# Order of the last chunk's table work and of GpSimd's second table set in a four-stage sequence kernel

## The chip, the cores and the metric

The kernel runs on one core of a Trainium2 chip. The metric is the device time of one execution in microseconds (us); three runs of the kernel before are shown, and one more execution was taken with the hardware profiler.

## The reference

An input `x` of 128 rows x 64 channels x 1024 steps goes through four additions, each with per-row conditions:

```
x = x + einsum('bct,bcd->bdt', x, W0[ids0])            # stage 0: a 64x64 mix per row
x = x + mask1 * (causal_conv(x, K1) + x * D1)          # stage 1: state-space convolution
x = x + x @ W2.T + bias + scale * (x @ A.T) @ B.T      # stage 2: 1024x1024 weights and a low-rank part
x = x + mask3 * (causal_conv(x * mask3, K3) + ...)     # stage 3: a second state-space convolution
K[h, l] = 2 * Re( sum_n Ct[h, n] * exp(dtA[h, n] * l) )   # 64 heads, 64 terms, 1024 steps, for each convolution
```

## The kernel before, in words

Work is split over channels into 16 groups (`NG`) of four (`HG`). The four engines, and the sync engine (SP) that issues most transfers, each run their own hand-written list of steps; a step waits on counting semaphores, so what stands in front of a step on its own engine delays it too.

**Opening.** Stage 0 runs over eight blocks and stores its result in DRAM (`x1_scratch`). Beside it, the tables of both convolutions are made in eight chunks of 16 heads. A chunk is: VectorE's `right_angles`, `left_angles` and `adv_angles` (multiply by steps, round off whole turns), ScalarE's `chunk_sines` (sines, then exponentials), VectorE's `combine_a` and `combine_b`, which end in the semaphore `tables_ready`; then the chunk's table is stored (`store_tab`, to `tab_scratch`) and TensorE's `sum_k` makes the first kernel samples of it. Chunks 0 to 6 are done within stage 0. The eighth (`NBLK - 1`) is spread: its right angles and step 3 of its sines come after stage 0, its left angles stand on VectorE between the first and the second `t_split_lo(0, n)` (line 2116), its sine steps 5 and 6 on ScalarE behind the four `t_split_hi(0, n)` (line 1582), its combining on VectorE behind the low-rank rows of group 0 (line 2153), its store on ScalarE's queue behind the second pair of PSUM reads (line 1606).

**Group 0.** Stage 1's sums leave PSUM by `take_half` on VectorE (line 2043), are split into two float16 parts (`x2_split_hi` on ScalarE L1482, `x2_split_lo` on VectorE L2063), and `t_rows` (L2101 to L2106, counted by the semaphore `t_made` up to 4) makes the four combinations that a fast matrix product of stage 2 takes. `t_split_hi` (L1532) and `t_split_lo` (L2110) split these; `t_split_lo` n lets SP load a quarter of the next group's `x1` from DRAM (`load_part(1, n)`, line 567). TensorE's `stage2(0)` goes in order: own blocks, `low_products` (L1044), the two mixed blocks (L1068, they wait for `t_hi` and `t_lo` 1), the low-rank terms (L1077, they wait for `low_hi` and `low_lo`, which come from VectorE's scaling L2145, ScalarE's L1594 and VectorE's L2149), two sum blocks, `sum_k(NBLK - 1, 3)` (L818, waits for `tables_ready`), and then the blocks with `t_parts[2]`, which wait for `s2_read` 5.

ScalarE's list in `body(0)` is: low-rank high part, four PSUM reads (`read_part`, L1540), the store of the table, the difference row (L1608), two `x1_split_hi(1, h)` (L1473, these wait for the loaded quarters), and only then the `read_part` that gives `s2_read` 5. Later in the same list come `bases_hi(0, 1)` and on VectorE `bases_lo(0, 1)` (L1950), which lets SP load the next kernel rows and GpSimd go on.

**GpSimd** makes the tables of each group and convolution in `make_tables(v, g)`: six small products (L718 to L726, 128x68) and seven large ones (L728 to L744, 128x1024 or 128x512). In `body(0)` it makes (0, 1), then (1, 0), of which the second large product waits for `u_lo`, that is `bases_lo(0, 1)`. Table (0, 1) waits for its loaded rows alone.

Of the kernel before, what the change touches and what calls it, by code (L numbers as in the profile page):

```python
# [36 lines left out]
NBLK = T // P  # L37
# [12 lines left out]
HG = 4  # L50
# [28 lines left out]
def build(nc, x, ids0, len1, ids2, len3, w0, ssm1, ssm3, w2, bias2, lora_a, lora_b, lora_s, out):  # L79
    with ExitStack() as ctx:  # L80
# [12 lines left out]
        tab_dram = nc.dram_tensor("tab_scratch", [2 * NG, P, TAB], F32).ap()  # L93
# [62 lines left out]
        tab = [t.rearrange("p (q n) -> p q n", q=HG) for t in (part_of(gbuf, 16, HG * TAB / 256), area(48, HG * TAB / 256))]  # L156
# [90 lines left out]
        tables_ready = sem("tables_ready")  # L247
# [267 lines left out]
        def _(sp):  # L515
# [92 lines left out]
                load_tab(1, 0, n)  # L608
            for part in range(NPART):
                sp.wait_ge(x1_stored[1][part], 16 * NBLK // 2)  # L610
            def turn_x3(g, h):
                for part, xx in enumerate((x3h, x3l)):
                    sp.dma_start_transpose(x3t[:, h % 2, part], xx[:, h].rearrange("p k b -> p (k b)")).then_inc(x3_turned[h], 16)
# [56 lines left out]
        def _(pool):  # L670
# [28 lines left out]
            def make_tables(v, g):  # L699

                n = made(v, g)
                pool.wait_ge(tab_loaded[v], 32 * (g + 1))
                if v == 1:

                    at_least(pool, c3_past, HG * g)
                elif made_ahead(v, g):
                    pool.wait_ge(s2_summed, NSUM * (g - 1))
                    pool.wait_ge(x3_lo, NBLK * (g - 1))
                m32 = m32_first if is_first(v, g) else m32_ahead if made_ahead(v, g) else m32_late
                u32, v32, tab_now = base_home(v, g), table_home(v, g), tab_home(v, g)  # L710
                v4 = v32[:, :, 0:2, :].rearrange("p h n (a j) -> p h (n a) j", j=TB)
                m4 = m32.rearrange("p h (a j) -> p h a j", j=TB)
                u4 = u32.rearrange("p h (a j) -> p h a j", j=TB)
                at_least(pool, v_made, 2 * n)
                re, im = [tab_now[:, TAB - (2 - k) * HG:TAB - (1 - k) * HG].rearrange("p (h o) -> p h o", o=1).to_broadcast([P, HG, TL])
                          for k in range(2)]
                l0, l1, l2, l3, tmp = [left_row(tab_now, k) for k in range(5)]
                ptt(l2, l0, re, ALU.mult).then_inc(left_parts, 1)  # L718
                ptt(tmp, l1, im, ALU.mult).then_inc(left_parts, 1)
                ptt(l3, l1, re, ALU.mult).then_inc(left_parts, 1)  # L720
                pool.wait_ge(left_parts, 6 * n + 3)
                ptt(l2, l2, tmp, ALU.add).then_inc(left_parts, 1)
                pool.wait_ge(left_parts, 6 * n + 4)
                ptt(tmp, l0, im, ALU.mult).then_inc(left_parts, 1)
                pool.wait_ge(left_parts, 6 * n + 5)
                ptt(l3, l3, tmp, ALU.subtract).then_inc(left_parts, 1)  # L726
                pool.wait_ge(left_parts, 6 * n + 6)
                ptt(m4, left_of(tab_now, 2), right_of(tab_now, 0), ALU.mult).then_inc(u_parts, 1)  # L728
                at_least(pool, u_lo, n)
                ptt(u4, left_of(tab_now, 3), right_of(tab_now, 1), ALU.mult).then_inc(u_parts, 1)  # L730
                pool.wait_ge(u_parts, 2 * n + 2)
                ptt(u4, u4, m4, ALU.add).then_inc(u_made, 1)
                pool.wait_ge(u_made, n + 1)
                if is_first(v, g):
                    pool.wait_ge(tab_stored[0], 16 * NBLK // 2)
                ptt(m4, left_of(tab_now, 0), right_of(tab_now, 0), ALU.mult).then_inc(v_parts, 1)
                at_least(pool, v_lo, n)
                ptt(v4, left_of(tab_now, 1), right_of(tab_now, 1), ALU.mult).then_inc(v_parts, 1)
                pool.wait_ge(v_parts, 2 * n + 2)
                ptt(v4, v4, m4, ALU.add).then_inc(v_made, 1)  # L740
                decay = tab_now[:, 0:2 * LEFT].rearrange("p (s h a) -> p h s a", s=2, a=TL)[:, :, :, TB:TL].to_broadcast([P, HG, 2, C])
                eye = twin[:, :].rearrange("p (o s n) -> p o s n", o=1, s=1).to_broadcast([P, HG, 2, C])
                d4 = (v32[:, :, 2, :] if v == 0 else v32[:, :, 2, ::-1]).rearrange("p h (s n) -> p h s n", s=2)
                ptt(d4, eye, decay, ALU.mult).then_inc(v_made, 1)  # L744
# [28 lines left out]
            def body(g, more2):  # L773
                if isinstance(g, int) and g == 0:
                    for part in range(NPART):
                        pool.wait_ge(x1_stored[0][part], 16 * NBLK // 2)
                    make_tables(0, 1)
                make_tables(1, g)
                if more2:
                    make_tables(0, g + 2)  # L780
# [481 lines left out]
        def _(act):  # L1262
# [16 lines left out]
            def store_tab(c, r):  # L1279

                act.wait_ge(tables_ready, c + 1)
                act.dma_start(tab_dram[bass.ds(c * HG, HG)].rearrange("q p n -> p q n"), tab[r]).then_inc(tab_stored[r], 16)
# [40 lines left out]
            def chunk_sines(c, r, step):  # L1323

                if step == 3:
                    act.wait_ge(table_angles, 2 * c + 1)
                    nc.scalar.activation(right_slot(r, 0), right_slot(r, 0), ACT.Sin, bias=phase_cos, scale=-TURN)
                    nc.scalar.activation(right_slot(r, 1), right_slot(r, 1), ACT.Sin, scale=-TURN)
                if step == 5:
                    act.wait_ge(table_angles, 2 * c + 2)  # L1330
                    nc.scalar.activation(left_slot(r, 0), left_slot(r, 0), ACT.Sin, bias=phase_own, scale=-TURN)
                    nc.scalar.activation(left_slot(r, 1), left_slot(r, 1), ACT.Sin, bias=phase_adv, scale=-TURN)
                if step == 6:
                    nc.scalar.activation(angle_r, angle_r, ACT.Exp)
                    nc.scalar.activation(angle_l, angle_l, ACT.Exp).then_inc(table_sines, 1)
# [243 lines left out]
                x2_split_hi(0, h)  # L1579
            for n in range(4):  # L1580
                t_split_hi(0, n)
            chunk_sines(NBLK - 1, 1, 5)
            chunk_sines(NBLK - 1, 1, 6)
            for part in range(NPART):
                act.wait_ge(x1_stored[0][part], 16 * NBLK // 2)
                act.wait_ge(x1_stored[1][part], 16 * NBLK // 2)
# [1 line left out]
            def body(g, more1, more2):  # L1588
# [14 lines left out]
                read_part(g, 0, MIX_AT[0], 2, NQ, 2, 3)  # L1603
                read_part(g, 1, MIX_AT[1], 2, NQ, 2, 4)
                if early:
                    store_tab(NBLK - 1, 1)
                act.wait_ge(low_diff, g + 1)
                nc.scalar.activation(lowdh, lowf.rearrange("p h b -> p (h b)")[:, 0:HW], ACT.Copy).then_inc(lowd_hi, 1)  # L1608
                if more1:
# [83 lines left out]
        def _(dve):  # L1693
# [164 lines left out]
            def left_angles(c, r):  # L1858
                table_link(tt(four(angle_l), param(c, 1, TL), left_steps, ALU.mult), c, 7)
                round_off(left_slot(r, 0), four(angle_l), quarter_own, half_own[:, 0:1], half_own[:, 1:2], c, 8)  # L1860

            def adv_angles(c, r):
                table_link(round_off(left_slot(r, 1), four(angle_l), quarter_adv, half_adv[:, 0:1], half_adv[:, 1:2], c, 10), c, 12)
                tt(four(angle_l), param(c, 0, TL), left_steps, ALU.mult).then_inc(table_angles, 1)

            def combine_a(c, r):
                dve.wait_ge(table_sines, c + 1)
                at_least(dve, k_summed, c)
                tt(right_slot(r, 0), right_slot(r, 0), four(angle_r), ALU.mult)
                tt(left_slot(r, 0), left_slot(r, 0), four(angle_l), ALU.mult)  # L1870
                table_link(tt(right_slot(r, 1), right_slot(r, 1), four(angle_r), ALU.mult), c, 13)
                table_link(tt(left_slot(r, 1), left_slot(r, 1), four(angle_l), ALU.mult), c, 14)
                nc.vector.tensor_copy(four(turn_r)[0:C, :, :, ::-1], right_slot(r, 0)[0:C])
                nc.vector.tensor_copy(four(turn_r)[C:2 * C, :, :, ::-1], right_slot(r, 1)[C:2 * C])
# [233 lines left out]
            def t_split_lo(g, n):  # L2108
                dve.wait_ge(t_hi, 4 * g + n + 1)
                stt(t_part(n, 1), t_region(n), XS / FS, t_part(n, 0), ALU.mult, ALU.subtract).then_inc(t_lo, 1)  # L2110

            t_rows(0)
            for n in range(4):
                t_split_lo(0, n)
                if n == 0:
                    left_angles(NBLK - 1, 1)
                    adv_angles(NBLK - 1, 1)

            def past_sum(g, h):

# [18 lines left out]
            def body(g, more1, more2):  # L2139
# [10 lines left out]
                dve.wait_ge(low_lo, g + 1)  # L2150
                tt(low_row[:, 0:HW], low_row[:, 0:HW], low_row[:, HW:2 * HW], ALU.subtract).then_inc(low_diff, 1)
                if early:
                    combine_a(NBLK - 1, 1)
                    combine_b(NBLK - 1, 1)
                for h in range(HG):
# [124 lines left out]
```

## Time and profile before

| what | us |
|---|---|
| three runs: lowest, median, highest | 1560.33, 1564.65, 1567.99 |
| profiled execution, its own time | 1560.88 |
| span of its instructions | 1558.9 |
| busy: TensorE, VectorE, ScalarE, GpSimd | 1492.1, 1230.2, 752.9, 633.3 |
| mean granted clock of TensorE, share of full speed | 0.987 |

The span runs from the first to the last instruction; the own time has some 2 us around it. Line numbers are those of the kernel before. Times of day in the rows ("at 261.42") are us from the start of the span.

### The profile page before, as it was taken

What the parts mean: (1) busy time and instruction counts of PE and PEld (TensorE: products, weight loads), DVE (VectorE), ACT (ScalarE), POOL (GpSimd) and SP (SyncE); (2) the same over time, 40 slices, a digit from 0 to 9 for tenths busy, and PEclk for the clock granted to TensorE, in tenths of its full rate; (3) what the DMA queues carried; (4) which work ended last, traced back from release to release, by engine and by line L of the source; (5) the groups of instructions that cost most, each with busy time, mean ns of one, the idle gap of its engine ahead of it and who ended that gap; (6) DMA issues with size and microseconds to landing.
All of it is one profiled execution on the core that took longest, in us unless ns stands there. A gap on an engine that the chain in (4) does not pass through costs nothing.

```text
span 1558.9 us, 36859 instructions
## 1 busy us (share of the span) xinstructions
PE 1492.1 (96%) x14983; PEld 1292.4 (83%) x14983; DVE 1230.2 (79%) x1479; ACT 752.9 (48%) x1105; POOL 633.3 (41%) x455
## 2 busy tenths in 40 slices
PE   7888697999999999999999999999999999999998
PEld 7877685788888888888888888888888888888887
DVE  8888669788787969696969696978787887969653
ACT  4555543554444545454545454535454444445433
POOL 1211046445454545454443535353535454545040
PEclk9999899999999999999999999999999999999999
DMA  8899985848483848484848566674848583858432
GB/s 286 302 377 387 368 290 158 188 112 216 89 232 80 235 90 225 99 224 92 221 106 196 136 174 159 146 187 119 195 114 208 99 231 88 223 85 230 99 135 69
DMA packets 437847, 283.43 MB, mean 182 GB/s; under 512 B 330536, under 2 KB 377136, under 8 KB 437680
## 3 DMA queue, kind: packets, MB, share of 16 engines
q1 hardware_dynamic: 388784, 175.35, 47.7%
q10 hardware_dynamic: 48928, 106.00, 19.6%
q8 instruction: 119, 1.95, 0.5%
q14 instruction: 16, 0.13, 0.0%
HBM read 159.20 MB, written 73.86 MB: 150 GB/s over the span
## 4 chain that ended last, share of the span: by engine, by line
PE 76%; DVE 10%; DMA 6%; issue 4%; ACT 3%; ACTq 0%; DVEq 0%; SPq 0%
PE ps L1068 35%; PE ps L978 8%; PE ps L1168 7%; DMA arena<-in_x_dram 5%; PE ps L1077 5%; PE ps L1044 5%; PE ps L1014 4%; PE ps L1181 3%; PE ps L869 3%; PE ps L988 3%; DVE arena L2066 3%; PE ps L797 1%; DVE gbuf L2057 1%; ACT arena L1564 1%; ACT arena L1484 1%
## 5 line engine op out<-in xcount | busy, mean ns | idle before, releaser
L1068 PE MATMUL ps<-arena,w2t 128*128 128x256 f16 x4608 | 524.2, 273 | 7.4 <-ACT arena L1532 5.1
L1068 PEld LDWEIGHTS ps<-arena,w2t 128*128 128x128 f16 x4608 | 451.7, 98 | 65.0 <-ACT arena L1532 5.6
L718 POOL TENSOR_TENSOR arena<-arena 128x68 f32<-128x68 f32 x31 | 27.7, 893 | 665.7 <-DVE arena L2130 396.7
L2173 DVE TENSOR_TENSOR arena<-arena 128x512 f16<-128x512 f32 x128 | 107.5, 840 | 113.8 <-ACT arena L1553 113.8
L1540 ACT ACTIVATE arena<-ps,biasx 128x256 f32<-128x256 f32 x256 | 103.4, 472 | 132.2 <-PE ps L1068 95.6
L869 PE MATMUL ps<-arena 128*128 128x128 f32 x976 | 128.3, 290 | 35.9 <-DMA arena<-in_x_dram 22.7
L1553 ACT ACTIVATE arena<-arena 128x512 f16<-128x512 f32 x128 | 80.6, 630 | 164.2 <-DVE arena L2169 163.2
L869 PEld LDWEIGHTS ps<-arena 128*128 128x128 f32 x976 | 120.6, 203 | 41.6 <-DMA arena<-in_x_dram 25.5
L2036 DVE SCALAR_TENSOR_TENSOR arena<-gbuf,arena 128x1024 f16<-128x1024 f32 x60 | 151.3, 2539 | 1.5 <-ACT arena L1473 1.5
L1168 PE MATMUL ps<-arena 128*128 128x256 f16 (+1 forms) x1536 | 137.1, 246 | 1.5 <-DVE gbuf L2057 0.5
L1168 PEld LDWEIGHTS ps<-arena 128*128 128x128 f16 x1536 | 122.1, 98 | 15.4 <-DVE gbuf L2057 5.1
L1014 PE MATMUL ps<-arena 128*128 128x512 f16 x720 | 126.8, 326 | 0.0
L1014 PEld LDWEIGHTS ps<-arena 128*128 128x128 f16 x720 | 69.2, 98 | 45.8
L1484 ACT ACTIVATE arena<-gbuf 128x1024 f16<-128x1024 f32 x60 | 63.3, 1055 | 78.2 <-DVE gbuf L2057 76.7
L2021 DVE SCALAR_TENSOR_TENSOR arena<-ps,arena 128x512 f16<-128x512 f32 x48 | 33.2, 692 | 79.4 <-ACT arena L1506 79.4
L730 POOL TENSOR_TENSOR arena<-arena 128x1024 f32<-128x1024 f32 x31 | 82.9, 2673 | 24.4 <-DVE arena L1950 24.4
L2066 DVE SCALAR_TENSOR_TENSOR arena<-gbuf,arena 128x1024 f16<-128x1024 f32 x60 | 91.9, 1550 | 0.0
L1068 PE MATMUL ps<-arena,gbuf 128*128 128x256 f16 x768 | 90.6, 275 | 0.0
L1044 PE MATMUL ps<-arena,at 128*128 128x512 f16 x384 | 85.5, 379 | 0.0
L1068 PEld LDWEIGHTS ps<-arena,gbuf 128*128 128x128 f16 x768 | 75.9, 99 | 9.6
L1564 ACT ACTIVATE arena<-arena 128x1024 f32<-128x1024 f16 x60 | 63.0, 1050 | 41.7 <-DVE arena L2130 41.7
L1532 ACT ACTIVATE arena<-gbuf 128x1024 f16<-128x1024 f32 x64 | 65.7, 1052 | 34.8 <-DVE gbuf L2102 33.6
(277 smaller groups left out, 2849.5 us busy)
## 6 DMA issues: line engine op xcount, KB each, us to landing
w2t<-w_scratch ACTq DMA_DIRECT2D x96, 512.0 KB, 4.4
out_dram<-arena SPq DMA_DIRECT2D x64, 512.0 KB, 2.8
arena<-in_x_dram SPq DMA_DIRECT2D x61, 512.0 KB, 9.0
gbuf<-x_scratch SPq DMA_DIRECT2D x60, 512.0 KB, 5.5
x_scratch<-arena ACTq DMA_DIRECT2D x25, 960.0 KB, 9.5
gbuf<-w_scratch ACTq DMA_DIRECT2D x32, 512.0 KB, 4.2
arena<-krow_scratch SPq DMA_DIRECT2D x31, 512.0 KB, 8.4
x_scratch<-arena SPq DMA_DIRECT2D x7, 960.0 KB, 7.1
```

The lines of the kernel that those rows point to most:

```text
L730: ptt(u4, left_of(tab_now, 3), right_of(tab_now, 1), ALU.mult).then_inc(u_parts, 1)
L869: mm = nc.tensor.matmul(ps[:, s, at0:at0 + P], x_slot(i, l)[:, j, t0:t0 + P], pick[:, i % 2 * 2 * STEPS + l * GPAIRS + j, :], start=True, ...
L978: mm = nc.tensor.matmul(o, ut_part(v, g, part)[:, 2 * h + blk, :], state_rows(split, h, 2 * k + blk), start=(h == 0 and q == 0 and blk == ...
L1014: nc.tensor.matmul(o, g1[:, h, part, d * P:(d + 1) * P], m, start=(d == 0 and q == 0), stop=False)
L1044: mm = nc.tensor.matmul(ps[:, 7, :], at[:, part, k, :], xx[:, :, k, :], start=(k == 0 and q == 0), stop=(k == NBLK - 1 and q == 2))
L1068: mm = nc.tensor.matmul(ps[:, bank, n * HW:(n + 1) * HW], weight(p, n, part, k), xx[:, :, k], start=(fresh and n == 0 and k == 0 and q == ...
L1168: nc.tensor.matmul(ps[:, bank, c0:c0 + w], xx[:, h, j, :], g3[:, h, part, g0:g0 + w], start=(j % 4 == 0 and xx is x3h and part == 0), stop ...
L1540: e = nc.scalar.activation(x3part[slot + p][:, n * HW:(n + 1) * HW], ps[:, bank, n * HW:(n + 1) * HW], ACT.Identity, bias=biasx[:, o:o + 1 ...
L1553: nc.scalar.activation(x3_quarter(x3h, h0, row), x3part[slot].rearrange("p (k h b) -> p k h b", k=2, h=2), ACT.Copy).then_inc(x3_hi, 1)
L2036: stt(batch_parts(lo[:, h]), x1_flat[:, :, h], XS / FS, batch_parts(hi[:, h]), ALU.mult, ALU.subtract).then_inc(x1_lo, 1)
L2066: stt(batch_parts(x2l[:, h]), x1_flat[:, :, h], XS / FS, batch_parts(x2h[:, h]), ALU.mult, ALU.subtract).then_inc(x2_lo, 1)
L2173: tt(x3_quarter(x3l, h0, row), x3part[slot].rearrange("p (k h b) -> p k h b", k=2, h=2), x3_quarter(x3h, h0, row), ALU.subtract).then_inc( ...
```

## The change

GpSimd's `make_tables(0, 1)` waits for all four sums of `t_rows(0)`. VectorE's left and advanced angles of the last chunk, and the fourth `t_split_lo(0, 3)`, go behind the low-rank rows. ScalarE's sine steps 5 and 6 go behind the four PSUM reads, into the place of the table's store; the store goes to SP, in front of the four loads `load_part(1, n)`.

```diff
@@ SP, before load_part(1, n)
                 sp.wait_ge(x1_stored[1][part], 16 * NBLK // 2)
+            sp.wait_ge(tables_ready, NBLK)
+            sp.dma_start(tab_dram[(NBLK - 1) * HG:NBLK * HG].rearrange("q p n -> p q n"), tab[1]).then_inc(tab_stored[1], 16)
+
@@ GpSimd, body(0)
                         pool.wait_ge(x1_stored[0][part], 16 * NBLK // 2)
+                    pool.wait_ge(t_made, 4)
                     make_tables(0, 1)
@@ ScalarE, before body(0)
             for n in range(4):
                 t_split_hi(0, n)
-            chunk_sines(NBLK - 1, 1, 5)
-            chunk_sines(NBLK - 1, 1, 6)
@@ ScalarE, body(0)
                 read_part(g, 1, MIX_AT[1], 2, NQ, 2, 4)
                 if early:
-                    store_tab(NBLK - 1, 1)
+                    chunk_sines(NBLK - 1, 1, 5)
+                    chunk_sines(NBLK - 1, 1, 6)
                 act.wait_ge(low_diff, g + 1)
@@ VectorE, before body(0)
             t_rows(0)
-            for n in range(4):
+            for n in range(3):
                 t_split_lo(0, n)
-                if n == 0:
-                    left_angles(NBLK - 1, 1)
-                    adv_angles(NBLK - 1, 1)
@@ VectorE, body(0)
                 tt(low_row[:, 0:HW], low_row[:, 0:HW], low_row[:, HW:2 * HW], ALU.subtract).then_inc(low_diff, 1)
                 if early:
+                    t_split_lo(0, 3)
+                    left_angles(NBLK - 1, 1)
+                    adv_angles(NBLK - 1, 1)
                     combine_a(NBLK - 1, 1)
                     combine_b(NBLK - 1, 1)
```

## Rows read from the trace of the kernel before

**Rows 1.** Windows of the later stretch: us, busy of each engine, clock, DMA share, GB/s

```profile
560.00:1400.00 840.00, 839.15 (x8564) 718.74 (x8562) 681.06 (x671) 409.50 (x573) 389.10 (x267) 1.00 0.66 156
```

**Rows 2.** Timeline of TensorE: start, us, line, out<-in, count, [idle before, releaser]

```profile
245.70 5.40 PE L1068 MATMUL ps<-arena,w2t 128*128 128x256 f16 x48 [1.38 <-DVE arena L2063]
...
261.42 7.80 PE L1068 MATMUL ps<-arena,w2t 128*128 128x256 f16 x48 [5.15 <-ACT arena L1532]
272.08 1.68 PE L1077 MATMUL ps<-gbuf,bt 128*128 128x256 f16 x12 [2.86 <-DVE gbuf L2149]
273.57 4.28 PE L1068 MATMUL ps<-arena,gbuf 128*128 128x256 f16 x24
...
281.29 2.79 PE L1068 MATMUL ps<-arena,w2t 128*128 128x256 f16 x24
...
307.39 2.74 PE L978 MATMUL ps<-arena 128*128 128x128 f16 x24 [2.98 <-ACT arena L1540]
```

**Rows 3.** Window of 2 us with the clock before its last two figures

```profile
264.00:266.00 2.00, 2.00 (x11) 1.40 (x10) 1.91 (x3) 0.00 (x0) 0.89 (x1) 0.50 0.61 132
```

**Rows 4.** Timeline of VectorE, 230 to 290 us

```profile
230.05 1.32 DVE L2049 SCALAR_TENSOR_TENSOR arena<-gbuf,arena 128x512 f16<-128x512 f32 x2
...
241.45 4.10 DVE L2063 SCALAR_TENSOR_TENSOR arena<-gbuf,arena 128x512 f16<-128x512 f32 x2
...
246.90 3.76 DVE L2063 SCALAR_TENSOR_TENSOR arena<-gbuf,arena 128x512 f16<-128x512 f32 x2
250.77 2.77 DVE L2101 TENSOR_TENSOR gbuf<-gbuf 128x1024 f32<-128x1024 f32 x1
253.46 3.37 DVE L2102 TENSOR_TENSOR gbuf<-gbuf 128x1024 f32<-128x1024 f32 x1
256.86 1.97 DVE L2104 TENSOR_TENSOR gbuf<-gbuf 128x1024 f32<-128x1024 f32 x1
258.86 1.23 DVE L2106 TENSOR_TENSOR gbuf<-gbuf 128x1024 f32<-128x1024 f32 x1
...
263.02 2.03 DVE L1842 TENSOR_SCALAR arena<-gbuf,small 128x272 f32<-128x272 f32 x1
...
269.79 0.68 DVE L2145 TENSOR_TENSOR gbuf<-ps,adapter_scale 128x512 f32<-128x512 f32 x1
...
271.97 0.42 DVE L2151 TENSOR_TENSOR gbuf<-gbuf 128x256 f32<-128x256 f32 x1
...
275.45 0.44 DVE L1882 TENSOR_TENSOR gbuf<-gbuf 128x272 f32<-128x272 f32 x1
...
288.00 1.21 DVE L1950 SCALAR_TENSOR_TENSOR arena<-arena 128x1024 f16<-128x1024 f32 x1
```

**Rows 5.** Timeline of GpSimd: group 0's set, and a later set with VectorE out of its way

```profile
252.53 3.21 POOL L740 TENSOR_TENSOR arena<-arena 128x1024 f32<-128x1024 f32 x1
255.71 2.04 POOL L744 TENSOR_TENSOR arena<-twin,arena 128x512 f32<-128x512 f32 x1
...
262.92 1.97 POOL L728 TENSOR_TENSOR arena<-arena 128x1024 f32<-128x1024 f32 x1
...
395.26 1.93 POOL L728 TENSOR_TENSOR arena<-arena 128x1024 f32<-128x1024 f32 x1
...
407.79 2.05 POOL L744 TENSOR_TENSOR arena<-twin,arena 128x512 f32<-128x512 f32 x1
```

**Rows 6.** Timeline of ScalarE: first and last of the four sine steps

```profile
266.50 0.52 ACT L1331 ACTIVATE arena<-arena,small 128x272 f32<-128x272 f32 x1 [4.38 <-DVE gbuf L1864]
...
269.05 0.41 ACT L1335 ACTIVATE gbuf<-gbuf 128x272 f32<-128x272 f32 x1
```

**Rows 7.** Chain of waits, 190 to 330 us: start, us, what

```profile
269.89 9.66 DMA gbuf<-x_scratch
```

**Rows 8.** DMA queues, 260 to 282 us (packets, MB, share of 16 engines), and L567's landings

```profile
q1 hardware_dynamic: 8256, 2.10, 48.7%
...
DMA to landing us min/median/max: 4.7/5.5/9.7
```

## The prediction, made before the changed kernel was run

> **What bounds the kernel now.** I read the windows first. From 560 to 1400 us TensorE is busy 839.15 of 840 us at full clock [rows 1], so the long loop has no slack: a shift before it is carried to the end, and only the passage from the opening into group 0, some 237 to 307 us, can change the time. TensorE's timeline there shows what is to be had [rows 2]: it stands 5.15 us before the mixed blocks at 261.42 and 2.86 us before the low-rank terms at 272.08. Each wait also costs clock: the granted clock is 0.50, the lower of its two levels (1.2 and 2.4 GHz), in the stretch behind the first [rows 3]; the 48 matmuls at 261.42 took 7.80 us where 48 of the same shape took 5.40, and 24 at 273.57 took 4.28 where 24 at 281.29 took 2.79 [rows 2]. So 5.15 + 2.4 + 2.86 + 1.5 = 11.9 us lie in these two places. Third, TensorE waits 2.98 us before 307.39 [rows 2], for PSUM reads that a chain of VectorE and ScalarE steps holds back, not for itself.
>
> VectorE's timeline says why the first wait is there [rows 4]. GpSimd's large products and VectorE's instructions with SBUF operands take turns: the tensor_scalar at 263.02 took 2.03 us and ended at 265.05, just behind GpSimd's L728, which ran from 262.92 to 264.89 [rows 5]; L2102 at 253.46 took 3.37 us and ended 1.1 us behind GpSimd's L740, which itself had been held to 3.21 us [rows 4, 5]. The turns alternate: in group 0's set of seven large products one such VectorE instruction lies between any two of them.
>
> **The change, part by part.**
>
> *GpSimd waits for the sums.* VectorE is alone until `t_rows` is done. The four L2063 need 2 x 1.32 (the price of two such at 230.05) in place of 4.10 + 3.76: 5.2 us less. The first three sums of `t_rows` need 3 x 1.23 (the fourth's price) in place of 2.77 + 3.37 + 1.97: 4.4 us less [rows 4]. So the sums end 9.6 us earlier, at 260.1 - 9.6 = 250.5, and with one split of 1.2 us `t_lo` 1 is there at 251.7. TensorE's own blocks wait 1.38 us less [rows 2], so the low-rank product ends at 256.3 - 1.4 = 254.9 and the mixed blocks follow at once: the first wait and its slow clock go. `make_tables(0, 1)` is 13 us later; its readers on ScalarE come at about 285 us before, and nobody else waits for it. `make_tables(1, 0)` is queued behind it, but is held anyway until `bases_lo(0, 1)` at 289.2 [rows 4].
>
> *Low-rank rows in front of the angles.* The rows from scaling to difference took 269.79 to 272.4, 2.6 us [rows 4]. They now start at 254.9 instead of 269.8, so the second wait of TensorE goes too: the terms are wanted when the mixed blocks end, 254.9 + 5.4 = 260.3.
>
> *But GpSimd now runs beside the low-rank rows and the angles.* It starts at 250.5. From the end of its L744 at 257.75 over the next set's six small products to the first large one at 262.92 it took 5.2 us between VectorE's instructions, so the first large one now starts at 255.7; from there to the start of L744 it needs 12.5 us by itself (395.26 to 407.79) [rows 5]. Between its seven large products, one VectorE instruction each gets through: the low half (0.7, as its neighbour L2145), the difference (0.42), `t_split_lo(0, 3)` (1.2) and three of the eight angle instructions. The eight took 5.2 us (from 261.3, the end of the split behind L2106, to the sines at 266.5), of which L1842's waiting was 1.7: 3.5 us clean, 1.3 for three [rows 4, 6]. So L744 starts and the third angle instruction ends at about 255.7 + 12.5 + 3.6 = 271.8. L2102 finished beside L744's first microsecond and L2104 waited only for its second [rows 4, 5]: I add 1.0 us for it, and 2.2 us for the five angle instructions left: 275.0.
>
> The Trainium skill ("SBUF — State Buffer", section "Who interferes with whom") has the pair of ports locked for a whole instruction where both engines read SBUF; L2102 and L744 overlapping speak against the whole for this product. By the page L744 would cost 1.0 us more than I take, and the sum below would be 16.1 instead of 15.1.
>
> *Sines and combining.* The sine steps took 266.50 to 269.46, 3.0 us [rows 6]; ScalarE's four reads in front of them are done by about 261 and cost nothing. Combining took 272.4 to 275.9, 3.5 us [rows 4]. So `tables_ready` comes at T = 275.0 + 3.0 + 3.5 = 281.5 us; before it was 275.9. TensorE comes to `sum_k` at about 254.9 + 5.4 + 1.5 + 5.4 = 267.2 and waits there.
>
> *The store on SP.* The store, moved from ScalarE's queue (0.4 us of issue, beside other work), now stands with its wait in front of the four `load_part(1, n)`. Before, these were released by the splits, between 261.3 and 269.9, and the last landed at 279.55 [rows 7]. Now none is issued before T. The four loads held the 16 engines for 0.487 x 22 = 10.7 us, 2.7 each, and the quickest landed 4.7 after its issue [rows 8], so 2.0 of it is start and completion; with 0.4 for the store's issue the last lands at T + 0.4 + 2.0 + 10.7 = T + 13.1 = 294.6, the third near T + 10.4. Behind the third come two `x1_split_hi` and the read that gives `s2_read` 5, together 3 us: TensorE goes on at about T + 13.4 = 294.9 where it went on at 281.29 before [rows 2]. From the last landing to the end of `bases_lo(0, 1)` it was 289.2 - 279.55 = 9.7 us [rows 4, 7]; those steps are unchanged, so it ends at T + 22.8 = 304.3, and what follows up to TensorE's restart at 307.39 is shifted alike: 304.3 - 289.2 = **15.1 us later**. TensorE by itself is not the limit: restart at 294.9, 19.7 us of blocks, 2.4 for a low clock after the long wait, 3.4 for the next two steps gives 320.4, under 307.4 + 15.1 = 322.5. Its third wait shrinks, which may give 1 us or so of clock back; I leave that out.
>
> Bounds of the unknown costs. The taking of turns: from no turns (T = 254.9 + 2.6 + 1.2 + 3.5 + 3.0 + 3.5 = 268.7) to all of them (281.5); I take all, since in the nearest rows it held without exception. The loads: from 13.1 behind T to 0.4 + 9.66 + 3 x 2.7 = 18.2, if the first takes as long as the slow one before and three follow at 2.7 each, and down to 11, if their packets go faster with no weight loads beside them; I take 13.1, since the other transfers that slowed the last load are ahead of T now.
>
> **Sum.** Gained 11.9 us at the two old waits, lost 27.0 at the new ones: +15.1 on the profiled execution's 1560.88, which gives 1576.0. The median of the runs stands 3.8 us above that execution, so for the median 1564.65 + 15.1 = 1579.75, 1580 in round numbers.
>
> **Rivals.**
>
> *VectorE keeps the port.* If its chained instructions win their turns, T = 268.7, `bases_lo` ends at 291.5 and the change costs 2.3 us: 1567. For it: the angle instructions follow each other within 0.1 us. Against it: L1842 in the same spot waited a whole product [rows 4, 5]. 0.20, with a partial form of it.
>
> *The loads take longer.* 18.2 in place of 13.1 gives +20.2, 1584.9. For it: the last load took 9.66 us though it was alone on its queue [rows 7]. Against: weight loads shared the engines then. 0.12.
>
> *Faster: the two old waits go and nothing takes their place.* TensorE gets back up to 11.9 us, 1552.8. It is decided at the moment that the last quarter of `x1` is loaded: to be 7.8 us faster, `bases_lo(0, 1)` must end by 281.4, so T must come by 258.6, or the loads must not wait for T. For it: the rows show the waits as plain idle time of the busiest engine. Against it: even with no turns T is 268.7, and every load stands behind it. 0.07.
>
> The forecast has 0.58; 0.03 is for what I don't see.
>
> **How the numbers follow.** The range goes from 1 us under the first rival (for the clock that I left out) to 1 us above the second, 1566 to 1586, and leaves out the faster case and the outer tails, under 2 in 10. Something like 0.5% of 1564.65, 7.8 us, is what a measurement can tell from no change: slower begins at 1572.5, which takes the forecast, the long loads and the partial forms, 0.73; within it 0.20; faster 0.07.
>
> **What would show it.** In the new trace VectorE's L2063 and L2101 to L2104 should stand at 0.66 and 1.23 us, the mixed blocks should start at about 255 with no wait, and the low-rank terms at about 260. The low half, the difference, the fourth split and three angle instructions should each end behind a GpSimd product; the last VectorE instruction of the combining should end near 281.5; `sum_k` and then the block at t_parts[2] should wait, with a restart of TensorE near 295 and a clock of 0.50 about it; `bases_lo(0, 1)` should end near 304. I am wrong if the combining ends by 272, or if the `x1` loads land within 8 us of it, or if the loop at 560 to 1400 us shows TensorE waiting.

## The result, and the profile of the changed kernel

Four runs of the changed kernel have a median of 1578.07 us (1577.49 to 1580.13), beside 1564.26 for four of the kernel before: a ratio of 1.0085, with a 95% interval of [1.0052, 1.0118], that is 8 to 18 us. It is slower by 13.8 us in the medians; the forecast was 15.1 slower, 1580. (The ratios here and below can differ by up to 0.001 from the quotient of the two medians beside them.)

The profiled execution took 1577.49, 16.6 more than that of before. First the page (span, then busy time of each engine, then the granted clock in 40 slices):

```profile
span 1575.5 us, 36859 instructions
...
PE 1490.9 (95%) x14983; PEld 1293.1 (82%) x14983; DVE 1221.8 (78%) x1479; ACT 753.1 (48%) x1105; POOL 628.9 (40%) x455
...
PEclk9998999699999999999999999999999999999999
```

VectorE is busy 8.4 us less and GpSimd 4.4 less, with the same number of instructions, and the kernel is still slower. Not all of that is the change's doing: 6.0 of VectorE's 8.4 lie in the opening, and in the stretch that the change touches it is busy 62.8 us (239.68 to 328.44) where it was busy 63.1 (237 to 312), GpSimd 39.6 where it was 42.8. What VectorE no longer waits at the sums it waits later. Next the windows, the long loop as in [rows 1], and 14 us of the opening:

```profile
560.00:1400.00 840.00, 839.12 (x8576) 719.05 (x8575) 671.74 (x665) 409.10 (x576) 385.79 (x270) 1.00 0.66 158
282.00:296.00 14.00, 1.04 (x32) 0.93 (x32) 1.25 (x2) 2.03 (x3) 0.00 (x0) 0.50 0.94 210
```

The loop is as it was. From 282 to 296 hardly any engine works (TensorE 1.04 us, VectorE 1.25, ScalarE 2.03, GpSimd nothing), while the DMA engines are 0.94 busy: the kernel waits for transfers there. TensorE's timeline, to be held against [rows 2]:

```profile
257.25 5.40 PE L1072 MATMUL ps<-arena,w2t 128*128 128x256 f16 x48
262.50 1.47 PE L1081 MATMUL ps<-gbuf,bt 128*128 128x256 f16 x12
...
282.03 1.04 PE L822 MATMUL ps<-gbuf 128*16 128x16 f32 x32 [12.82 <-DVE gbuf L1885]
296.85 4.13 PE L1072 MATMUL ps<-arena,w2t 128*128 128x256 f16 x24 [13.78 <-ACT arena L1544]
...
323.83 2.74 PE L982 MATMUL ps<-arena 128*128 128x128 f16 x24 [2.54 <-ACT arena L1544]
```

The mixed blocks (257.25) and the low-rank terms (262.50) start without a wait and at full clock: 5.40 us for 48 matmuls, as forecast. Then TensorE waits 12.82 us before `sum_k` and 13.78 before the block behind it, and that block takes 4.13 us where 24 such took 2.79 before; the clock was 0.50 in the window just above. VectorE, against [rows 4]:

```profile
240.76 0.69 DVE L2024 SCALAR_TENSOR_TENSOR gbuf<-ps,gbuf 128x512 f16<-128x512 f32 x1 [1.36 <-ACT gbuf L1510]
...
246.65 1.32 DVE L2066 SCALAR_TENSOR_TENSOR arena<-gbuf,arena 128x512 f16<-128x512 f32 x2
248.07 1.23 DVE L2104 TENSOR_TENSOR gbuf<-gbuf 128x1024 f32<-128x1024 f32 x1
...
260.50 2.04 DVE L2151 TENSOR_TENSOR gbuf<-gbuf 128x256 f32<-128x256 f32 x1
262.46 3.37 DVE L2113 SCALAR_TENSOR_TENSOR arena<-gbuf,arena 128x1024 f16<-128x1024 f32 x1
265.76 2.16 DVE L1862 TENSOR_TENSOR gbuf<-gbuf,steps 128x272 f32<-128x272 f32 x1
267.96 1.91 DVE L1845 TENSOR_SCALAR arena<-gbuf,small 128x272 f32<-128x272 f32 x1
269.90 2.52 DVE L1846 SCALAR_TENSOR_TENSOR arena<-arena,gbuf 128x272 f32<-128x272 f32 x1
...
281.53 0.45 DVE L1885 TENSOR_TENSOR gbuf<-gbuf 128x272 f32<-128x272 f32 x1
```

Up to the sums everything is at its own price (1.32 for two, 1.23). From the low half on, VectorE runs beside GpSimd's large products, and instructions of 0.4 us take 1.9 to 2.5. GpSimd, SP and ScalarE in the same stretch:

```profile
257.99 1.94 POOL L731 TENSOR_TENSOR arena<-arena 128x1024 f32<-128x1024 f32 x1
...
269.79 2.34 POOL L743 TENSOR_TENSOR arena<-arena 128x1024 f32<-128x1024 f32 x1
272.08 1.25 POOL L747 TENSOR_TENSOR arena<-twin,arena 128x512 f32<-128x512 f32 x1
```
```profile
282.06 0.40 SPq L612 DMA_DIRECT2D tab_scratch<-arena  x1
282.50 8.72 SPq L567 DMA_DIRECT2D gbuf<-x_scratch  x4
```
```profile
293.97 1.06 ACT L1477 ACTIVATE arena<-gbuf 128x1024 f16<-128x1024 f32 x1 [15.30 <-DMA gbuf<-x_scratch]
```

The tables are ready at 281.98; SP issues the store 0.1 us later and then, one behind another, the four loads of `x1`; ScalarE waits until 293.97 for the third of them. That is the chain the prediction named.

**One comparison for all kernels below.** The opening up to group 0 moves by a few us from one execution to the next: the split at 240.76 above (L2024) began at 238.08 in the kernel before, but at 235.55 in a kernel (`e7`) with the same code up to there. So I count from the start of this split (the "state split" of some expectations below). "T" is the end of the last instruction of the tables' combining, then the end of `bases_lo(0, 1)`, then TensorE's restart in the recurrence ([rows 2], 307.39):

| kernel | T | `bases_lo` ends | restart | restart against before |
|---|---|---|---|---|
| before | 37.8 | 51.1 | 69.3 | |
| after | 41.2 | 64.9 | 83.1 | +13.8 |
| `e4`: before, store on SP | 37.1 | 60.5 | 78.7 | +9.4 |
| `e3`: after, GpSimd doesn't wait | 39.7 | 62.7 | 80.9 | +11.6 |
| `e1`: after, store behind the loads | 41.3 | 53.9 | 72.1 | +2.8 |
| `e7`: after, GpSimd waits for T | 30.5 | 57.2 | 75.4 | +6.1 |
| `e2`: before, GpSimd waits for the sums | 38.6 | 51.1 | 69.3 | 0.0 |
| `e8`: before, GpSimd waits for the low-rank difference | 26.4 | 46.7 | 65.7 | -3.7 |
| `e5`: `e8`, store on SP behind the loads | 26.4 | 46.7 | 65.6 | -3.7 |
| `e6`: `e5`, two table steps later | 26.3 | 46.7 | 68.0 | -1.3 |

From the restart to the end of the span it is 1251.7 us after and 1251.5 before, so the 16.6 us between the two profiled executions are 13.8 from this passage and 2.7 from the opening; the medians, with an interval of 8 to 18 us, can't tell the two apart. The table has one profiled execution of each kernel (`e5` two, which agree within 0.02 us in each column).

### The profile page after: what moved, and what is told of

The parts are those of the page before. It is cut to its first block, busy times and chain, and to the rows that moved or that the text cites. A ratio compares the mean times of both kernels' runs of the same rounds, so it can differ in the third digit from the quotient of the medians.

```text
span 1575.5 us, 36859 instructions
## 1 busy us (share of the span) xinstructions
PE 1490.9 (95%) x14983; PEld 1293.1 (82%) x14983; DVE 1221.8 (78%) x1479; ACT 753.1 (48%) x1105; POOL 628.9 (40%) x455
## 4 chain that ended last, share of the span: by engine, by line
PE 76%; DVE 11%; DMA 5%; issue 4%; ACT 3%; ACTq 0%; SPq 0%; DVEq 0%
PE ps L1072 35%; PE ps L982 8%; PE ps L1172 6%; PE ps L1048 5%; PE ps L1081 5%; PE ps L1018 4%; DMA arena<-in_x_dram 4%; PE ps L1185 3%; PE ps L873 3%; PE ps L992 3%; DVE arena L2069 2%; PE ps L801 1%; DVE gbuf L2060 1%; ACT arena L1568 1%; ACT arena L1488 1%
## 5 line engine op out<-in xcount | busy, mean ns | idle before, releaser
L1072 PE MATMUL ps<-arena,w2t 128*128 128x256 f16 x4608 | 523.0, 273 | 14.6 <-ACT arena L1544 13.8
L1488 ACT ACTIVATE arena<-gbuf 128x1024 f16<-128x1024 f32 x60 | 63.3, 1054 | 78.5 <-DVE gbuf L2060 77.0
L2024 DVE SCALAR_TENSOR_TENSOR arena<-ps,arena 128x512 f16<-128x512 f32 x48 | 33.2, 692 | 79.3 <-ACT arena L1510 79.3
L733 POOL TENSOR_TENSOR arena<-arena 128x1024 f32<-128x1024 f32 x31 | 82.9, 2674 | 27.8 <-DVE arena L1953 27.8
L1568 ACT ACTIVATE arena<-arena 128x1024 f32<-128x1024 f16 x60 | 63.1, 1051 | 40.4 <-DVE arena L2130 40.4
L743 POOL TENSOR_TENSOR arena<-arena 128x1024 f32<-128x1024 f32 x31 | 78.2, 2521 | 2.4
```

The lines of the kernel that those rows point to most:

```text
L1072: mm = nc.tensor.matmul(ps[:, bank, n * HW:(n + 1) * HW], weight(p, n, part, k), xx[:, :, k], start=(fresh and n == 0 and k == 0 and q == ...
```

## The experiments

Two theories. **Mine**, the "queue theory" of the expectations: nearly all of the loss is SP's queue, the loads of `x1` standing behind a wait for the tables, and T is itself late because VectorE and GpSimd take turns. **The rival**, the "turns theory": the turns alone do it, and the loads would be hidden anyway.

**e1: the loads first.** In the kernel after, on SP:

```
-            sp.wait_ge(tables_ready, NBLK)
-            sp.dma_start(tab_dram[(NBLK - 1) * HG:NBLK * HG].rearrange("q p n -> p q n"), tab[1]).then_inc(tab_stored[1], 16)
...
             for n in range(4):
                 load_part(1, n)
+            sp.wait_ge(tables_ready, NBLK)
+            sp.dma_start(tab_dram[(NBLK - 1) * HG:NBLK * HG].rearrange("q p n -> p q n"), tab[1]).then_inc(tab_stored[1], 16)
```

> The changed kernel with SP's wait and the store put behind the four x1 loads. Queue theory (the loads standing behind the wait for tables_ready are the cost): the loads are issued with the splits, some 17 to 30 us earlier; TensorE waits for tables_ready once, at sum_k, and goes on into the next block within 2 us of it; what is left is the store's landing in front of ScalarE's splits, so about +2 us on the kernel before, 1566. Turns theory (the cost is that the angles take turns with GpSimd, so that tables_ready is late, wherever the loads stand): still +8 us or more, 1572 and up. tables_ready itself is where it was in both.

1567.01 against 1562.66: 1.0021 [1.0005, 1.0036]. T is where it was in the kernel after, but the restart is only 2.8 us late: 11.0 of the 13.8 are gone with two statements moved. TensorE, then SP, then ScalarE of `e1`:

```profile
281.91 1.04 PE L822 MATMUL ps<-gbuf 128*16 128x16 f32 x32 [12.85 <-DVE gbuf L1885]
282.88 4.16 PE L1072 MATMUL ps<-arena,w2t 128*128 128x256 f16 x24
```
```profile
254.05 12.06 SPq L567 DMA_DIRECT2D gbuf<-x_scratch  x4
281.89 0.38 SPq L624 DMA_DIRECT2D tab_scratch<-arena  x1
```
```profile
287.10 0.63 ACT L1557 ACTIVATE arena<-arena 128x512 f16<-128x512 f32 x1 [4.26 <-DMA tab_scratch<-arena]
```

The wait of 12.85 before `sum_k` stays, most of it the price of the turns (`e7` below: 2.14); the second one, 13.78, is gone, since the loads went out at 254. The store landing is the next thing waited for: `split_hi3` on ScalarE stands 4.26 us for it.

**e4: the store on SP alone.** The kernel before, with only the queue changed:

```
+            sp.wait_ge(tables_ready, NBLK)
+            sp.dma_start(tab_dram[(NBLK - 1) * HG:NBLK * HG].rearrange("q p n -> p q n"), tab[1]).then_inc(tab_stored[1], 16)
             def turn_x3(g, h):
...
-                if early:
-                    store_tab(NBLK - 1, 1)
```

> The kernel before with only the store moved from ScalarE to SP, in front of the four x1 loads with its wait. Queue theory: tables_ready at 275.9 as before, the loads 24 us in front of the end of bases_lo(0, 1) as in the changed kernel, where it ended at 289.2: 275.9 + 23.7 - 289.2 = +10.4 us, 1574.7. Turns theory: no change, 1564.

1572.46 against 1562.66: 1.0064 [1.0041, 1.0087]. The restart is 9.4 us late, from one store on another queue. TensorE of `e4` still has its old waits, though not all at the same blocks: 4.41 before its own blocks (1.38 before), none before the mixed blocks (5.15), 4.63 before the low-rank terms (2.86), together 9.0 where they were 9.4. It has the new one of 7.96 besides; SP issues the loads at 277.79 and no earlier:

```profile
250.78 7.62 PE L1070 MATMUL ps<-arena,w2t 128*128 128x256 f16 x48 [4.41 <-DVE arena L2063]
...
273.45 2.72 PE L1079 MATMUL ps<-gbuf,bt 128*128 128x256 f16 x12 [4.63 <-DVE gbuf L2149]
...
291.83 4.96 PE L1070 MATMUL ps<-arena,w2t 128*128 128x256 f16 x24 [7.96 <-ACT arena L1542]
```
```profile
277.79 8.83 SPq L567 DMA_DIRECT2D gbuf<-x_scratch  x4
```

The rival falls: the loads weren't hidden.

**e3: the change without GpSimd's wait.** In the kernel after, one line taken out:

```
-                    pool.wait_ge(t_made, 4)
                     make_tables(0, 1)
```

> The changed kernel without GpSimd's wait. The angles then meet no large product of GpSimd, but come after the low-rank rows, and the loads stand behind tables_ready. Queue theory: sums at 260 as before, tables_ready some 2 us later than before, everything behind it as in the changed kernel: +12 to +13 us, 1577. Turns theory: with the turns gone from the angles most of the loss goes, +3 us, 1567.

1572.64 against 1562.66: 1.0057 [1.0037, 1.0078]; restart at +11.6. TensorE of `e3`:

```profile
262.60 8.04 PE L1071 MATMUL ps<-arena,w2t 128*128 128x256 f16 x48 [5.13 <-ACT arena L1535]
279.75 0.96 PE L821 MATMUL ps<-gbuf 128*16 128x16 f32 x32 [2.57 <-DVE gbuf L1884]
293.90 5.13 PE L1071 MATMUL ps<-arena,w2t 128*128 128x256 f16 x24 [13.19 <-ACT arena L1543]
```

The first old wait is back (5.13, with the slow clock behind it: 8.04 for 48), and `sum_k` waits 2.57 instead of 12.82. Yet T moves only 1.5 us, from 41.2 to 39.7. What the wait gains for the sums, the products take back beside the low-rank rows and the angles. So the parts add up in this order: queue +9.4; the new order on VectorE and ScalarE, +2.2 more; GpSimd's wait, +2.2 more. In another order they need not: GpSimd's wait alone (`e2`, next) costs nothing.

**e2: GpSimd's wait alone.** The kernel before with the one line added:

```
+                    pool.wait_ge(t_made, 4)
                     make_tables(0, 1)
```

> The kernel before with GpSimd's wait for the four sums alone. Queue theory: VectorE's sums end 9.6 us earlier, the wait of 5.15 us before the mixed blocks goes with its slow clock, the splits and low-rank rows then take turns with GpSimd, so that the low-rank terms wait some 7 us at TensorE in place of 2.9; tables_ready about where it was or 1 us earlier, x1 loads 4 to 5 us earlier. Total -4 us, 1560. Turns theory: the turns are only moved from the sums to the splits, 0 to +3 us, 1564 to 1567.

I had expected some 4 us of gain. 1563.25 against 1562.66: 1.0005 [0.9989, 1.0021], and the restart is at 0.0. A miss. VectorE and TensorE of `e2`:

```profile
249.65 1.22 DVE L2107 TENSOR_TENSOR gbuf<-gbuf 128x1024 f32<-128x1024 f32 x1
...
254.69 1.91 DVE L1845 TENSOR_SCALAR arena<-arena,small 128x272 f32<-128x272 f32 x1
256.64 2.05 DVE L1865 TENSOR_TENSOR gbuf<-gbuf,steps 128x272 f32<-128x272 f32 x1
258.61 9.10 DVE L2111 SCALAR_TENSOR_TENSOR arena<-gbuf,arena 128x1024 f16<-128x1024 f32 x3
...
274.21 1.87 DVE L1879 COPY arena<-gbuf 128x32 f32<-128x32 f32 x1
```
```profile
270.61 2.72 PE L1078 MATMUL ps<-gbuf,bt 128*128 128x256 f16 x12 [10.04 <-DVE gbuf L2150]
```

The sums end at 12.2 from the split, 9.8 earlier than before (22.0). Then the two last angle instructions (1.91 and 2.05) and the three splits (9.10, where `e8` below takes 3.49) are held, and late in the combining even a copy of 128x32 takes 1.87. T ends up 0.8 later than before. The two old waits of TensorE have turned into one of 10.04. The products cost VectorE as much behind the sums as beside them: over the whole passage it is busy 64.3 us in `e2` and 63.1 before.

**e7: GpSimd waits for the tables.** In the kernel after:

```
-                    pool.wait_ge(t_made, 4)
+                    pool.wait_ge(tables_ready, NBLK)
```

> The changed kernel with GpSimd's wait for tables_ready instead of the four sums, so that no product of GpSimd runs beside the splits, the low-rank rows, the angles and the combining. If the lateness of tables_ready in the changed kernel is the taking of turns, its place behind the state split L2021 falls from 41.2 us to about 30.6, the loads stay chained 23.7 us behind it, and the whole comes to +3 us on the kernel before, 1566. If the new order of VectorE is the cause and not the turns, tables_ready stays past 38 and the loss past +10 us.

1568.01 against 1563.83: 1.0022 [1.0004, 1.0039]; restart at +6.1. T is at 30.5, where 30.6 was expected, so the turns are worth 10.7 us of T in the kernel after; VectorE is busy 56.4 us in the passage instead of 62.8. The whole, though, was expected at +3. TensorE, then VectorE:

```profile
266.13 0.96 PE L822 MATMUL ps<-gbuf 128*16 128x16 f32 x32 [2.14 <-DVE gbuf L1885]
280.26 4.83 PE L1072 MATMUL ps<-arena,w2t 128*128 128x256 f16 x24 [13.16 <-ACT arena L1544]
```
```profile
280.57 2.77 DVE L2039 SCALAR_TENSOR_TENSOR arena<-gbuf,arena 128x1024 f16<-128x1024 f32 x1
...
288.93 1.90 DVE L1892 TENSOR_TENSOR gbuf<-gbuf,d_row 16x16 f32<-16x16 f32 x1
```

Of the 10.7 only 7.7 arrive: the products now lie beside the splits of `x1` (2.77 instead of 1.22) and the small product of 16x16 (1.90 instead of 0.17), which were free of them before. The wait for the loads is 13.16, as long as ever: with the queue as the change has it, even a T 7.3 us earlier than in the kernel before leaves the restart 6.1 late.

**e8: the kernel before and one line, at another place.** The end of VectorE's low-rank rows is the last point that TensorE's two old waits depend on:

```
+                    pool.wait_ge(low_diff, 1)
                     make_tables(0, 1)
```

> The kernel before with one edit alone: GpSimd's first set in body(0) waits for the low-rank difference. The store stays on ScalarE. If what gained in the own order was GpSimd's keeping out of the way until that difference, this one stands where that one did, 2 to 3 us below the kernel before, 1561; if the store's move to SP behind the loads was needed, it is back at the kernel before, 1564.

("The own order" is `e5`, below.) 1558.45 against 1563.77: 0.9973 [0.9958, 0.9987], that is 2 to 7 us below the kernel before, and below the kernel after. TensorE, VectorE and ScalarE of `e8`:

```profile
260.93 1.47 PE L1078 MATMUL ps<-gbuf,bt 128*128 128x256 f16 x12 [0.44 <-DVE gbuf L2150]
...
286.30 5.30 PE L1069 MATMUL ps<-arena,w2t 128*128 128x256 f16 x24 [7.21 <-DMA w2t<-w_scratch]
```
```profile
255.23 3.49 DVE L2111 SCALAR_TENSOR_TENSOR arena<-gbuf,arena 128x1024 f16<-128x1024 f32 x3
...
276.05 5.63 DVE L2037 SCALAR_TENSOR_TENSOR arena<-gbuf,arena 128x1024 f16<-128x1024 f32 x2
```
```profile
282.63 1.48 ACT L1499 ACTIVATE arena<-arena 128x1536 f16<-128x1536 f32 x1 [3.68 <-POOL arena L744]
```

The old waits are gone but for 0.44 us and T is 11.4 earlier, but the restart gains only 3.7. Two `x1` splits take 5.63 beside the products; and TensorE waits 7.21 us for a weight load, which ScalarE issues only at 282.63, behind its `table_hi(0, 1)`, and that waits 3.68 us for GpSimd's last product. That wait is the next thing in TensorE's way; `e6` shows that it isn't the only one.

**e5, e5_again: the same with the store on SP, behind the loads.**

```
             for n in range(4):
                 load_part(1, n)
+            sp.wait_ge(tables_ready, NBLK)
+            sp.dma_start(tab_dram[(NBLK - 1) * HG:NBLK * HG].rearrange("q p n -> p q n"), tab[1]).then_inc(tab_stored[1], 16)
...
-                if early:
-                    store_tab(NBLK - 1, 1)
...
+                    pool.wait_ge(low_diff, 1)
                     make_tables(0, 1)
```

> The kernel before (angles between the first two splits) with GpSimd's wait put on the low-rank difference, and the store on SP behind the four loads. Queue and turns theory: no turns until the difference, which comes 23.3 us behind the state split L2021 (34.3 before); tables_ready at about 27.5 (37.8 before); x1 loads early; then ScalarE and VectorE wait for GpSimd's finished table (0, 1), some 43 us behind that split, and the passage ends about 6 us earlier than before: 1557. A rival: GpSimd's tables, started 20 us later than before, hold ScalarE's table_hi(0, 1) past the place where it stood, and the time is as before or more.

> The own order again (angles as before, GpSimd waiting for the difference, store on SP behind the loads), on the same chip as the one-edit version, to see the difference of the two and whether the 2.6 us below the kernel before come again.

1561.19 against 1563.83, 0.9973 [0.9952, 0.9995]; the second time 1559.95 against 1563.77, 0.9976 [0.9960, 0.9991]. T came where it was expected (26.4 for 27.5), the restart gained 3.7 instead of 6: GpSimd's later tables hold `table_hi(0, 1)`, as the rival in the expectation had it, but don't eat up the whole gain. The restart is at -3.7, as in `e8`. Behind the loads the store's queue changes nothing that these runs can tell. From the restart to the end of the span, though, the two profiled executions take 1254.1 and 1253.2 us, `e8` 1252.2 and the kernel before 1251.5; so part of the 3.7 is lost again behind the passage, and why is not shown.

**e6: two table steps out of the way.** In `e5`, ScalarE's and VectorE's parts of the table moved back:

```
                     bases_hi(0, 1)
-                    table_hi(0, 1)
...
                 split_hi3(g, 3, 2, NQ + 2, 3)
+                if early:
+                    table_hi(0, 1)
...
                     bases_lo(0, 1)
-                    table_lo(0, 1)
...
                 lo3(3, 2, NQ + 2, 3)
+                if early:
+                    table_lo(0, 1)
```

> The same, with ScalarE's table_hi(0, 1) and VectorE's table_lo(0, 1) moved behind the fourth split_hi3 and lo3, where GpSimd's table is finished. If the wait for that table limits the kernel above, this one ends 2 to 4 us earlier than it, 1554; if not, the same time.

1561.73 against 1563.83: 0.9994 [0.9970, 1.0018]. A miss: it was to be 2 to 4 us below `e5`, and the gain of `e5` can't be seen any more. TensorE and VectorE of `e6`:

```profile
303.54 2.74 PE L981 MATMUL ps<-arena 128*128 128x128 f16 x24 [8.04 <-ACT arena L1543]
```
```profile
290.79 3.48 DVE L2016 SCALAR_TENSOR_TENSOR arena<-arena 128x1536 f16<-128x1536 f32 x1
```

The wait of 7.21 for the weight is gone (1.06 is the longest for one), but TensorE now waits 8.04 at the restart: VectorE's half of the table (3.48 beside GpSimd, where it took 1.74) stands in the chain to it. `bases_lo` is at 46.7 as in `e8`, the restart 2.3 later. What stays open is whether GpSimd's set cut in two, or that one weight load issued ahead of `table_hi`, keeps the gain; neither was tried.

## Why the prediction was right, and by how much its steps were off

**Bound, and the two old waits.** Right: the loop is unchanged, the waits of 5.15 and 2.86 us and their slow clock are gone, and the sums run at the price that I took from their free neighbours.

**The turns, T.** I took all of them, by [rows 4, 5], and the rows bore it out: each of the six VectorE instructions from the low half on ends behind a product. T was forecast 43.4 us from the split (281.5 - 238.1) and came at 41.2. The term that was off is "12.5 us by itself plus 3.6": from the first large product to the start of L747 it took 14.1 (257.99 to 272.08), not 16.1. The 12.5 stands: by themselves the six products take 1.93 us each but for the third and the sixth, which take 2.35, together 12.4. After, they took 1.94, 2.39, 2.42, 2.79, 2.12 and 2.34, together 14.0. So VectorE's turns held GpSimd for 1.6 us and not 3.6. Five of the six lie in front of L747 (the sixth ended 0.34 us into it), and each holds a product for less than the VectorE instruction takes by itself: the 1.22 of `t_split_lo(0, 3)` ended 1.00 us into L739 and held it for 0.86. The rest of T's working was within 0.4 us in each part. The first rival, VectorE keeping its turns, gave T = 268.7, 30.6 from the split: that is `e7`'s T, and not that of the change.

**L744's first microsecond.** I read [rows 4, 5] as overlap: L2102 ended 1.1 us after L744 began. The last set of the kernel before shows what the product takes with no VectorE instruction near it:

```profile
1507.39 2.35 POOL L740 TENSOR_TENSOR arena<-arena 128x1024 f32<-128x1024 f32 x1
1509.70 1.06 POOL L744 TENSOR_TENSOR arena<-twin,arena 128x512 f32<-128x512 f32 x1
```

So 1.0 of the 2.04 us in [rows 5] was waiting. (The later set's 2.05 is no clean price either: an L2066 of VectorE ended 1.14 us into it.) After, the same product (L747) took 1.25 us, beside a neighbour that ended 0.34 us into it; in `e8` it took 2.03, and its neighbour ended at 281.68, 1.12 into it. In all three cases the time held is the neighbour's stretch but for some 0.15 us. The Trainium skill ("SBUF — State Buffer", section "Who interferes with whom") has the port pair locked for the whole instruction, and the measured rows agree with it, but for that 0.15 us, where my reading of one row did not. What I made of it, 16.1, rested on two whole microseconds for L744; with the 1.25 that it took, the product and the five angles come to 3.3 us (272.08 to 275.39). I had 3.2, from a wrong reading that happened to give nearly the product's own time: luck.

**The store on SP.** Right in kind, and shown by `e4` and `e1`. The third load was forecast at T + 10.4 and landed at T + 12.0; TensorE's block behind `sum_k` was forecast at T + 13.4 and started at T + 14.9; `bases_lo` at T + 22.8 and was at T + 23.7. The DMA view of after, 282 to 296 us (columns as in [rows 8]), and the loads' landings:

```profile
q1 hardware_dynamic: 8784, 2.65, 86.0%
...
gbuf<-x_scratch SPq DMA_DIRECT2D x4, 512.0 KB, 7.2
tab_scratch<-arena SPq DMA_DIRECT2D x1, 544.0 KB, 5.2
```
```profile
DMA to landing us min/median/max: 6.2/7.2/8.1
```

The queue's packets took 0.860 x 14 = 12.0 us of 16 engines, against the 10.7 that I took from [rows 8]. Its 2.65 MB are the loads' 2.10 and the store's 0.55: I had counted 0.4 us for the store's issue and nothing for its 544 KB, which go first. That accounts for 1.3 of the third load's 1.6 us, by this count; no run takes the store away by itself.

**The sum.** +15.1 forecast, +13.8 measured, from T 2.2 earlier and the stretch behind it 0.9 longer: 15.1 - 2.2 + 0.9 = 13.8. The errors have opposite signs, so that the forecast came within 1.3 us is in part luck; either alone would have stayed in the range. The 27.0 us lost at TensorE were the 15.1 plus the 11.9, not a sum of rows: the rows show 12.82 + 13.78 of waiting and 1.3 of slow clock, 27.9, and a gain of 1.4 before its own blocks besides the 11.9. The rival "nothing takes their place" asked for T by 258.6 or loads that don't wait for T; `e8` has the latter and, at -3.7, half the gain that it asked for.

## What to carry to other kernels

A wait put in front of transfers on one engine's list is a wait for all of them (9.4 us in `e4`): before moving a store, list what follows it there and when each was issued so far. Where two engines exclude each other, pushing one set of work behind the other's first items only moved the collision here (`e2`); it gained when the set started behind the last item that the busiest engine waits for (`e8`), and then the next reader of that set must be looked at. Relief counted at one place (here 9.8 us at the sums) is worth nothing until it is followed to the next step that every chain shares.

## What was not expected of the hardware

- GpSimd's large products and VectorE's instructions with all operands in SBUF alternated one for one in the stretches shown here, whatever VectorE's instruction was: beside products of about 1.9 us, a 128x272 tensor_scalar took 1.91 instead of 0.36, a 16x16 tensor_tensor 1.90 instead of 0.17, and a 128x32 copy 1.87 instead of 0.18. The smallest instructions lose most. An instruction that reads PSUM was not held: L2170 at 269.82 of `e8`, 128x512, took 0.68 us beside such a product, as it does elsewhere.
- A duration in the profile includes the time that an instruction is held: 1.06 and 2.05 us are the same GpSimd product of 128x512 elements.
- Holding GpSimd back some 10 us longer, until the low-rank difference instead of the sums, turned a gain of nothing (1.0005 [0.9989, 1.0021]) into one that can be measured (0.9973 [0.9958, 0.9987]).
